# Window attention and a merge convolution on one core: the output projection multiplies rounded parts and remainders, merge pieces sit in other slots, and the steps at a change of image leave VectorE

## What is computed

```python
qkv = conv1x1(gn(x))                        # 192 -> 3*192 channels
wins = 8x8 windows of qkv                   # N = 64 tokens, 6 heads of 32 channels
o = irfft2(rfft2(q * scale) * rfft2(k))     # per channel, over the 8x8 window
attn = softmax(o @ v.T + bias)              # bias: one 6x64x64 table, from a small network
y = attn @ v                                # back to (B, C, H, W)
x = x + einsum('bchw,oc->bohw', y, proj_w) + proj_b        # end of layer 0
z = gn(x); z = z + laplacian3x3(z)
x = x + einsum(z, merge_w) + merge_b        # end of layer 1, 1x1
```

## Time and profile before

| what | value |
|---|---|
| median of 3 runs | 5898.05 us (5894.93 to 5898.69) |
| the profiled execution | 5900.44 us, of which the span of instructions 5898.6 us |
| PE busy | 5629.3 us (95%), 91644 matrix instructions |
| PEld | 4715.9 us (80%) |
| DVE | 4388.0 us (74%) |
| ACT | 3320.2 us (56%) |
| POOL | 3326.2 us (56%) |
| the chain of waits that ended last, by engine | PE 80%, ACT 9%, DVE 9%, issue 2% |
| mean granted PE clock, as a share of 2.4 GHz | 0.987 |

### The profile page before, as it was taken

How to read it: one execution, slowest core, us unless ns; L and a number is a source line. 1 busy time by engine, 2 the same in 40 slices (tenths; PEclk the granted TensorE clock), 3 DMA queues, 4 the chain that set the end, 5 groups by cost and what they waited for, 6 DMA issues and landing times.

```text
span 5898.6 us, 207339 instructions
## 1 busy us (share of the span) xinstructions
PE 5629.3 (95%) x91644; PEld 4715.9 (80%) x91644; DVE 4388.0 (74%) x7534; ACT 3320.2 (56%) x6404; POOL 3326.2 (56%) x2342
## 2 busy tenths in 40 slices
PE   7999999999999999999999999999999999999977
PEld 5888788888888888887788878888888888888854
DVE  5777777787777777777777778777787787776754
ACT  3666655555555555555555655555555555555522
POOL 1333346665666655665566655665656666666643
PEclk9999999999999999999999999999999999999988
DMA  4222133323333233332333333333333322232245
GB/s 133 74 59 59 56 80 107 106 75 101 98 105 106 78 99 102 107 102 73 101 107 109 91 87 95 103 109 86 91 98 108 107 77 77 82 85 78 80 107 135
DMA packets 392497, 550.51 MB, mean 93 GB/s; under 512 B 24822, under 2 KB 284601, under 8 KB 391610
## 3 DMA queue, kind: packets, MB, share of 16 engines
q1 hardware_dynamic: 391612, 537.24, 32.3%
HBM read 335.82 MB, written 201.33 MB: 91 GB/s over the span
## 4 chain that ended last, share of the span: by engine, by line
PE 80%; ACT 9%; DVE 9%; issue 2%; POOL 0%; SPq 0%; DMA 0%; DVEq 0%; POOLq 0%; ACTq 0%
PE b_q L540 22%; PE b_t L638 7%; PE b_s L656 7%; PE b_q L624 7%; PE b_t L614 6%; PE b_s L488 4%; PE b_t L596 3%; PE b_s L490 3%; PE b_s L547 3%; PE b_s L550 3%; PE b_s L501 3%; ACT qkh L983 2%; PE b_s L499 2%; ACT probs L1056 2%; PE b_s L559 2%; ACT probsT L983 2%
## 5 line engine op out<-in xcount | busy, mean ns | idle before, releaser
L1133 POOL TENSOR_TENSOR probs<-probs,srec 128x768 f32<-128x768 f32 x512 | 881.7, 1722 | 1678.8 <-DVE srec L966 1678.8
L1120 POOL TENSOR_TENSOR probs<-probs,smax 128x768 f32<-128x768 f32 x512 | 755.0, 1475 | 603.9 <-DVE smax L926 603.4
L983 ACT ACTIVATE vs<-b_q 128x192 f32<-128x192 f32 x1024 | 339.7, 332 | 1282.2 <-PE b_q L540 1282.2
L915 DVE TENSOR_TENSOR qkl<-b_q,qkh 128x384 fp32r<-128x384 f32 x1024 | 570.2, 557 | 588.4 <-ACT qkh L983 556.3
L921 DVE TENSOR_TENSOR probs<-b_s,posb 128x768 f32<-128x768 f32 x512 | 490.3, 958 | 676.4 <-PE b_s L656 675.1
L540 PE MATMUL b_q<-wnh,xh 128*128 128x288 f32 x2048 | 703.6, 344 | 68.3 <-DVE qkl L915 65.6
L540 PE MATMUL b_q<-wnl,xh 128*128 128x288 f32 x2048 | 606.8, 296 | 0.0
L540 PE MATMUL b_q<-wnl,xhl 128*128 128x288 f32 x2048 | 605.8, 296 | 0.0
L540 PE MATMUL b_q<-wnh,xl 128*128 128x288 f32 x2048 | 605.7, 296 | 0.0
L540 PE MATMUL b_q<-wnh,xhb 128*128 128x288 f32 x2048 | 605.0, 295 | 0.0
L1095 POOL TENSOR_TENSOR dg<-late 128x645 f32<-128x645 f32 x352 | 563.0, 1599 | 64.3 <-DMA late<-x_dram 50.5
(11 more groups left out here) (159 smaller groups left out, 13871.1 us busy)
## 6 DMA issues: line engine op xcount, KB each, us to landing
ld<-in_x SPq DMA_DIRECT2D x192, 512.0 KB, 4.6
late<-x_dram SPq DMA_DIRECT2D x112, 640.0 KB, 5.1
xs<-in_x SPq DMA_DIRECT2D x128, 512.0 KB, 5.5
x_dram<-late SPq DMA_DIRECT2D x128, 512.0 KB, 2.9
out<-late SPq DMA_DIRECT2D x128, 512.0 KB, 2.9
late<-x_dram SPq DMA_DIRECT2D x240, 192.0 KB, 5.8
xs<-in_x SPq DMA_DIRECT2D x128, 256.0 KB, 5.7
x_dram<-late SPq DMA_DIRECT2D x128, 256.0 KB, 3.6
```

What stands on the lines that cost most here:

```text
L915: V.tensor_tensor(qkl[:, i % 2, :], q_out, qkh[:, i % 2, :].bitcast(F32), ALU.subtract).then_inc(lo_out, 1)
L983: return A.activation(o, i, ACT.Copy)
L1120: P.tensor_tensor(probs[:, i % 2, :, :], probs[:, i % 2, :, :], smax[:, i % 2, :].unsqueeze(2).broadcast_to([128, 12, N]), ALU.subtract).t ...
L1133: P.tensor_tensor(probs[:, i % 2, :, :], probs[:, i % 2, :, :], srec[:, i % 2, :].unsqueeze(2).broadcast_to([128, 12, N]), ALU.mult).then_ ...
```

## The change

Four parts. (1) The projection works like qkv: its weights `wph`, `wpl` and y (`yh`, `yl`) are split into an FP32R part and a remainder, and each of two output halves (`b_r[:, 0:256]`, `b_r[:, 256:512]`, the second for output channels 64 to 191) is five FP32R multiplications with 256 columns. `yb` holds the last 64 channels, rounded parts in rows 0 to 63 and remainders in rows 64 to 127. ACT copies yT (4 groups now, heads 4 and 5 of both pairs in the same rows), then makes `yh` and the upper half of `yb` at the end of its double; POOL makes `yl` and the lower half of `yb` after that. PE waits for `yh_out` and `yl_done`. (2) The pieces stand in slots 0, 1, 2, 4, 5, 6, and the norm jobs in slots 3 and 7. (3) The steps at a change of image go to ACT and POOL, one in each slot; DVE keeps the reciprocals, the statistics and one row of a remainder. ACT also fills the borders. (4) POOL subtracts the maxima ahead of its stencil work, not behind it.

```diff
-PIECES = 6
+PIECE_SLOTS = (0, 1, 2, 4, 5, 6)
+LAST_SLOT = PIECE_SLOTS[-1]
...
-            if at_blk == 1 and 1 <= img <= B:
-                return (("mean", "dev")[ph - 6], img - 1, 0)
-            if at_blk == 2 and ph == 6 and 1 <= img <= B:
-                return ("mbias", img - 1, 0)
+            if at_blk == 1 and ph == 7 and 1 <= img <= B:
+                return ("mean", img - 1, 0)
+            if at_blk == 2 and 1 <= img <= B:
+                return (("dev", "mbias")[ph // 4], img - 1, 0)
             if at_blk == 12 and 0 <= img < B - 1:
-                return (("gmean", "gspread")[ph - 6], img + 1, 0)
+                return (("gmean", "gspread")[ph // 4], img + 1, 0)
             if at_blk == 14 and 0 <= img < B - 1:
-                return ("bias", img + 1, ph - 6)
+                return ("bias", img + 1, ph // 4)
...
-                m_wait(pe, it - 2 if it > ALONE else it - 1)
+                m_wait(pe, it - 2 if it > ALONE and it % 4 in (1, 2) else it - 1)
...
-            def project_a():
-                o = b_r[:, 0:256]
-                mm(o, wp[:, 0, :], yT[:, 0:2, :, :].rearrange("p i w (r c) -> p r (i w) c", c=WS),
-                   start=True, stop=False)
-                for i in range(2):
-                    mm(o.rearrange("p (r i w c) -> p i r w c", r=WS, i=2, w=2)[:, i], wp[:, 2 + i, :], rest,
-                       start=False, stop=(i == 1))
-
-            def project_b():
-                o = b_r[:, 256:384]
-                for i in range(2):
-                    out_rows = slice(i * CB, (i + 1) * CB)
-                    mm(o[out_rows], wp[:, 1, out_rows], yT[:, i, :, :].rearrange("p w (r c) -> p r w c", c=WS),
-                       start=True, stop=False, skip_group_check=True)
-                mm(o, wp[:, 4, :], rest, start=False, stop=True, skip_group_check=True).then_inc(proj_mm, 1)
+            def project(o, lo, n):
+                up = lo + 128
+                moving = [t[:, :, :, :].rearrange("p i w (r c) -> p r (i w) c", c=WS) for t in (yh, yl, yb)]
+                mm(o, wph[:, 0, lo:up], moving[0], start=True, stop=False)
+                mm(o, wpl[:, 0, lo:up], moving[0], start=False, stop=False)
+                mm(o, wpl[0:CB, 1, lo:up], moving[2][0:CB], start=False, stop=False)
+                pe.wait_ge(yl_done, 2 * n)
+                mm(o, wph[:, 0, lo:up], moving[1], start=False, stop=False)
+                return mm(o, wph[:, 1, lo:up], moving[2], start=False, stop=True)
...
-                                q, c = (h * HD, i * N) if h < 4 else (i * N + (h - 4) * HD, 2 * N)
+                                q, c = (h * HD, i * N) if h < 4 else ((h - 4) * HD, (2 + i) * N)
...
+                if pair(3):
+                    act.wait_ge(yT_out, pair(3)[1])
+                    copy(yh[:, :, :, :], yT[:, 0:2, :, :])
+                    copy(yb[0:CB, :, :, :], yT[0:CB, 2:4, :, :]).then_inc(yh_out, 1)
...
+                if pair(3):
+                    pool.wait_ge(yh_out, pair(3)[1])
+                    P.tensor_tensor(yl[:, :, :, :], yT[:, 0:2, :, :], yh[:, :, :, :].bitcast(F32), ALU.subtract).then_inc(yl_done, 1)
+                    pool.wait_ge(yl_done, 2 * pair(3)[1] - 1)
+                    P.tensor_tensor(yb[CB:128, :, :, :], yT[0:CB, 2:4, :, :], yb[0:CB, :, :, :].bitcast(F32),
+                                    ALU.subtract).then_inc(yl_done, 1)
+                    pool.wait_ge(yl_done, 2 * pair(3)[1])
...
-                if blk >= 0 and img + 1 < B and c == 13:
-                    if ph == 1:
-                        group_root()
-                    elif ph == 2:
-                        scaled()
-                    elif ph == 3:
-                        rounded((img + 1) % 2)
-                    elif ph == 4:
-                        remainder((img + 1) % 2)
-                    elif ph == 5:
-                        minus_mean()
+                if blk >= 0 and img + 1 < B and c == 13 and ph == 2:
+                    dve.wait_ge(g1_sd, img + 1)
+                    V.reciprocal(cst[:, 4, :], cst[:, 3, :]).then_inc(g1_rec, 1)
...
+            def weights(blk, ph):
...
+                    if (c, ph) == (13, 0):
+                        act.wait_ge(a_read, a_count[8 * (blk - 1) + 7])
+                        A.activation(cst[:, 3, :], cst[:, 1, :], ACT.Sqrt).then_inc(g1_sd, 1)
+                    elif c == 13 and ph > 2:
+                        t = ph // 2 - 2
+                        act.wait_ge(g1_root, b)
+                        act.wait_ge(lo_w, 2 * (b - 1))
+                        A.activation(wn[:, t, :], wq[:, t, :], ACT.Copy, scale=cst[:, 4, t:t + 1]).then_inc(wn_done, 1)
```

More of the change, by code:

```diff
@@ L119, in proj_blocks @@
     t = weight.T
[L120 to L123 removed]
+    return np.concatenate([t[:CA], np.concatenate([t[CA:], t[CA:]])], axis=1)
 def program(nc, x, out, w):
@@ L816, in m_result @@
                 kind, at, p = task
-                if kind == "piece" and it >= ALONE and p < 4:
+                if act_reads(it):
                     return
@@ L1006, in a_result @@
+                if kind == "bias" and p == 1:
+                    act.wait_ge(bias_w, 2 * v - 1)
+                if kind == "mean" and v:
+                    act.wait_ge(border_w, border_count[NS * v - 1])
+                act.wait_ge(m_mm, m_count[it])
+                if kind == "piece":
                     A.activation(res_a[:, v % 2, p * 256:(p + 1) * 256], m_region(it)[:, 0:256], ACT.Identity,
                                  bias=mc[:, v // NS % 2, 0:1]).then_inc(a_read, 1)
+                elif kind == "gmean":
+                    copy(gst[:, 3:4], m_out[:, 0:1]).then_inc(a_read, 1)
+                elif kind == "gspread":
+                    copy(cst[:, 0:2, :], m_out[:, 0:4].rearrange("p (t f) -> p f t", t=2)).then_inc(a_read, 1)
+                elif kind == "bias":
+                    first, second = (slice(row, row + 1) for row in BIAS_ROWS)
+                    lo, up = p * QKV // 2, (p + 1) * QKV // 2
+                    copy(wnh[first, v % 2, 1, lo:up], m_out[first, 0:QKV // 2])
+                    copy(biashi[second, :], m_out[second, 0:QKV // 2])
+                    copy(biasrow[second, :], m_out[second, 0:QKV // 2]).then_inc(a_read, 1)
+                elif kind == "mean":
+                    copy(sm[:, 2:4, :], m_out[:, 0:4].rearrange("p (t f) -> p f t", t=2)).then_inc(a_read, 1)
+                else:
+                    A.activation(sm[:, 5, 0:1], m_out[:, 0:1], ACT.Identity, bias=sm[:, 7, 0:1])
+                    A.activation(sm[:, 5, 1:2], m_out[:, 2:3], ACT.Identity, bias=sm[:, 7, 1:2]).then_inc(a_read, 1)
@@ new lines, in border @@
+            def border(v):
+                s = v % NS
+                if 3 <= s < NS - 1:
+                    return
+                act.wait_ge(a_read, a_count[8 * (NS * (v // NS + 1) + 1) + 7])
+                if v >= 3:
+                    act.wait_ge(m_mm, m_count[8 * (v - 3 + MERGE_LAG) + LAST_SLOT])
+                if s < 3:
+                    for t, src in ((0, src_a), (1, src_b)):
+                        last = A.activation(src[v % 3][:, :, 0:PW:PW - 1],
+                                            ones[:, 0:1].unsqueeze(2).broadcast_to([128, (10, 6)[t], 2]), ACT.Copy,
+                                            scale=sm[:, 2, t:t + 1])
+                if s in (0, NS - 1):
+                    for t, src, part, row in ((0, src_a, slice(0, 128), (0, 9)[s > 0]),
+                                              (1, src_b, (slice(0, CB), slice(CB, 128))[s > 0], (0, 5)[s > 0])):
+                        last = A.activation(src[v % 3][part, row, 1:W + 1], ones[part, :], ACT.Copy,
+                                            scale=sm[part, 2, t:t + 1])
+                last.then_inc(border_w, 1)
@@ L1084, in _ @@
             P.memset(sm[:, :, :], 0.0)
+            for k, value in enumerate((-0.5, 1.5, EPS, -1.0)):
+                P.memset(fixed[:, k, :], value)
             P.memset(ones[:, :], 1.0).then_inc(ones_done, 1)
+            chain = [0]
             d = dg[:, :].rearrange("p (r c) -> p r c", c=W + 1)
```

242 lines of the change are left out of this document (139 added, 103 removed).

## The result

The changed kernel takes 5921.94 us (median of 7 runs, 5909.11 to 5925.26) against 5897.38 us (7 runs, 5893.64 to 5902.44) for the kernel before on the same chip: ratio 1.0039, 95% interval 1.0028 to 1.0051. It is slower by 0.4%, where I had forecast 0.6% faster.

The account below looks back on a forecast made before the run. PE, busy 95% of the span and 80% of the chain, was taken as the bound. Blocks +42, change of image -85, rest +6 gave -37 from 5900.4, 5863; the median lies 2.4 lower: 5861 us, range 5745 to 5940.

Parts of the forecast that it names:

- the section on the slots: Steady block of four doubles: 42.49 us becomes 42.9, 0.4 more in each of 109 blocks, +42 us.
- the price of a detour to 64 rows: Projection's third multiplication of each five, on 64 input rows: two row changes cost PE 0.39 us, twice per double.
- The column price: Each FP32R projection multiplication of 256 columns takes 0.118 us on PE (0.108 to 0.133); rival at 0.133: 10%.
- The waits for `qkl`: PE's idle before qkv's second half in the double without a piece goes; with the wait before y, 0.8 us per block.
- No wait for `yl` that counts: POOL's two remainders, 0.65 us each, finish 0.65 us before PE's projection wants them.
- The end: Last 17 blocks and last norm stages: +12 for piece 3 waiting on ACT, -6 for better spread, +6 us together.
- the change of image: Between images, PE's waits for DVE's long list mostly go: 65 us plus about 20, -85 us (bounds -103 to -50).
- The terms for PE's own jobs: At each change of image, 8.4 of the 24 us are PE's own jobs (`bias`, `mean`, `dev`, small rest) and stay.
- the projection's price in a double: PE's projection work per double goes from 1.66 to 1.96 us, a loss of 0.30 (0.20 to 0.45).
- the block's gain from the slots and the rest: Filled even slots remove waits before qkv's second half and y in one double: 0.8 us less per block.
- that POOL isn't late: POOL's remainders and the subtraction of maxima queued behind them finish in time; rival that POOL is late, about 6270 us: 8%.

Follow-up runs that it names:

- release mended: Changed kernel with SyncE's loads of x1 rows let go when the projection of double 1 is done: 5837.06 us, 0.9894 of the kernel before.
- the four times of release: Changed kernel with x1 loads let go at end of double 0 (5846 us), slot 2 (unmodified, 5922), projection of double 1 (5837) or after slot 4 (5889).
- the two kernels with one PE list and one release: Kernel before plus only the new projection, 6586.72 us (has gaps); the same plus POOL's subtraction ahead of the stencil, 5980.94 us (no such gaps).

## Why the prediction was wrong

**The step that failed** is in the section on the slots: "The block becomes 42.49 - 0.8 + 4 x 0.30 = 42.9". It took PE's work in a steady block as PE's multiplications and the semaphores they wait for, and moved only PE's, ACT's and POOL's side of the slots. SP's list counts the same slots. The move let it load x1 rows half a double earlier, and the median block became 43.45 (changed) where 42.68 (release mended) was due: 82 us of span, 84 us in the medians of 108 blocks. That is the whole change of sign. I had named no rival of this kind; "a transfer that comes at another time" was missing.

The early release costs by its stops (some 60 us in the parts of doubles) and by the 1.2 GHz behind them (some 15).

**Right, as far as the runs show:** the price of a detour to 64 rows, 0.39 us. The column price (0.115 to 0.12 measured, 0.118 taken). The waits for `qkl`, gone. No wait for `yl` that counts: 1.4 us from 1640 to 5615, at 0.74 us for each remainder where I took 0.65. The end, +8 against +6.

**Right in the sum, in part by luck:** the change of image, -86 against -85. An image takes 16 blocks + 10 us, where 11 was forecast and 24 had been. I put all of it down to the steps that leave DVE. POOL's order alone, which the sum has nowhere, takes 29 us of it off in the kernel before, and what the steps add to that in the changed kernel no run takes apart. (The terms for PE's own jobs add up to 8.3 us, not 8.4.)

**Right in kind, off in size:** the projection's price in a double (0.24, 0.04, 0.31 and 0.02, not 0.30 in all four) and the block's gain from the slots and the rest (0.45, not 0.8; 0.71 with POOL's order in both kernels); together +17 us in 108 blocks, not +42 in 109. That the price is near 0.30 in two doubles is luck. The sum set 1.66, pieces of the chain, against 1.96, distances between starts. By distances the projection goes from 1.49 to 2.22 in double 0, since the first step of each five is 0.21 and not 0.12, and the shorter steps into and out of it, for which the sum has no term, take most of that back.

**Right for the wrong reason:** that POOL isn't late. I looked at whether `yl` comes in time for PE, and named the subtraction behind it. In the change it stands first, and it isn't late. I put no price on that order. Its total is nothing in the kernel before, and 606 us once the remainders are there.

**Not settled:** No run holds the fetch back without a burst, or leaves the burst away; that the fetch stands behind queued data rests on the packets' times, on the four times of release, and on the two kernels with one PE list and one release, of which only the one whose dense part lies inside the burst has gaps. Nor does a run part the slots from POOL's order.

## What to carry to other kernels

When slots or numbered jobs move, search every engine's list for counts of them, the DMA issuer's too; a wait by count doesn't move with its job. When a new burst time and idle time of kind "issue" in a stream of small instructions come together, look at the instruction queue in the same microseconds and move the burst's release to where its end falls on long instructions. After a stop, look at the granted clock of the microseconds behind it: the stop may cost more than its length. A reordering whose total is nothing alone may be what another part of the change stands on, and may hide a gain and a loss, so cost the parts together and look at the blocks as well as the total.

## What was not expected of the hardware

- PE's instructions come in portions of 256 (16384 bytes, packets that take 0.9 to 1.4 us and a few up to 1.9, some 8 us apart), and PE can run dry: in the 24 gaps the next multiplication follows 2.3 to 3.0 us after the packet's start, 1.2 to 1.7 us after its end. The Trainium skill (Runtime: NRT & Kernel Launch, Instruction fetch mechanics) says that each engine's instructions are refilled in blocks of 16 KiB, 256 instructions, while the block before is executed, and that crossing a boundary is mostly hidden. By the size the trace agrees. Hidden it is in all but some 30 of 510 fetches of the changed kernel from 1640 to 5615; the rest, with the burst in the way, cost up to 2.3 us each.
- Of such a packet behind a burst, in the gap shown: none in 4.9 us of data at 167 to 401 GB/s, then one within 0.1 us of its end.
- Behind stops of 1.5 to 2.3 us inside a stream that PE otherwise fills, the granted clock often was 0.50 for 3.4 us, once for 6.8 (1.2 in place of 2.4 GHz): twelve such stretches in the changed kernel from block 19 to 126, none with the release mended. Five stops of 2.1 to 2.3 us had none behind them.
- FP32R multiplications of 256 columns start 0.115 to 0.12 us apart on the same rows; a change from 128 rows to 64 adds 0.09, the change back 0.19 and then 0.10.
- The step from a float32 job into the projection is 0.20 to 0.22 us when its first multiplication is float32 and 0.03 when it is FP32R; counted to the start of the next part, a piece goes from 0.86 to 0.68 and the transposes of the probabilities from 0.75 to 0.57, though the steps inside them stay.
